# Layer 0 scan: half of the inputs from the eighth state on made by TensorE, an eighth by GpSimd

## The reference

```
def step(h, inp):
    u_t, dt_t, B_t, C_t = inp
    dA = jnp.exp(-dt_t[..., None] * A)
    h = dA * h + (dt_t * u_t)[..., None] * B_t[:, None, :]
    y = jnp.einsum('bdn,bn->bd', h, C_t)
    return (h, y)
```

## Time and profile before

| | |
|---|---|
| median of 3 runs | 1251.55 us (1249.97 to 1255.73) |
| the profiled execution | 1258.5 us |
| its span | 1257.2 us |
| mean granted PE clock | 0.861 of full speed |
| first scan instruction starts at | 84.5 us of the span |
| last scan instruction starts at | 311.5 us |
| busy over the span | PE 915.5, DVE 899.7, ACT 578.6, POOL 547.4 us |

### The profile page before, as it was taken

How to read it: one execution, slowest core, us unless ns; L and a number is a source line. 1 busy time by engine, 2 the same in 40 slices (tenths; PEclk the granted TensorE clock), 3 DMA queues, 4 the chain that set the end, 5 groups by cost and what they waited for, 6 DMA issues and landing times.

```text
span 1257.2 us, 18690 instructions
## 1 busy us (share of the span) xinstructions
PE 915.5 (73%) x5207; PEld 533.2 (42%) x5207; DVE 899.7 (72%) x1700; ACT 578.6 (46%) x1232; POOL 547.4 (44%) x553
## 2 busy tenths in 40 slices
PE   6977787888666866678889888679893850558782
PEld 3522234333344552222223322469893530547682
DVE  6679999999999377877887871754455589972223
ACT  3478663665132443146776668334342740223232
POOL 2068995999401323201112211245534585235643
PEclk9879898999877988679998999679996775669896
DMA  8000000000000301311110100511102000011113
GB/s 294 1 1 1 1 0 1 1 1 1 1 0 1 134 1 53 98 27 27 27 28 27 27 2 2 201 62 35 39 27 78 1 0 1 9 42 36 41 33 113
DMA packets 28018, 46.32 MB, mean 37 GB/s; under 512 B 8721, under 2 KB 16409, under 8 KB 26897
## 3 DMA queue, kind: packets, MB, share of 16 engines
q1 hardware_dynamic: 22672, 34.67, 8.6%
q0 software_dynamic: 4096, 8.35, 2.2%
q10 hardware_dynamic: 1152, 2.10, 0.4%
HBM read 34.46 MB, written 12.58 MB: 37 GB/s over the span
## 4 chain that ended last, share of the span: by engine, by line
PE 39%; DVE 30%; issue 11%; ACT 8%; POOL 5%; DMA 3%; another core or an unknown queue 2%; SPq 1%; DVEq 0%; ACTq 0%; POOLq 0%
PE ps L2798 9%; PE ps L2807 5%; PE ps L1821 5%; PE ps L1803 4%; DVE sb_hs L756 3%; POOL sb_gs L926 3%; DVE sb_l_mxp L1935 2%; PE ps L1748 2%; DVE sb_xn L168 2%; DVE sb_stats L145 2%; ACT sb_l_rc L2228 1%; PE ps L1756 1%; ACT sb_l_pT L1878 1%; DVE ps L718 1%
## 5 line engine op out<-in xcount | busy, mean ns | idle before, releaser
L1935 DVE TENSOR_REDUCE sb_l_mxp<-ps 128x2 f32<-128x1024 f32 (+3 forms) x152 | 171.5, 1163 | 41.5 <-PE ps L1748 40.2
L926 POOL TENSOR_TENSOR sb_gs<-sb_hs,sb_xp 128x512 f32<-128x512 f32 x128 | 163.2, 1294 | 23.2 <-DVE sb_hs L756 21.1
L1878 ACT ACTIVATE sb_l_pT<-ps 128x512 f32<-128x512 f32 (+3 forms) x256 | 111.4, 521 | 76.8 <-PE ps L1803 75.7
L2798 PE MATMUL ps<-sb_hT,sb_f_shared 128*128 x936 | 127.5, 288 | 13.6 <-ACT sb_f_shared L2815 6.8
L605 PE MATMUL ps<-sb_gs,sb_ident 128*128 128x512 f32 x256 | 133.8, 605 | 1.0 <-POOL sb_gs L926 0.7
L2798 PEld LDWEIGHTS ps<-sb_hT,sb_f_shared 128*128 128x128 f32 x936 | 116.6, 200 | 22.2 <-issue 22.2
L2868 DVE SCALAR_TENSOR_TENSOR sb_f_rows<-ps,sb_f_mask,sb_f_rows 128x128 f32 x78 | 27.4, 351 | 116.6 <-PE ps L2807 57.0
L1803 PE MATMUL ps<-sb_l_qk 51*128 51x512 bf16 (+3 forms) x384 | 89.3, 335 | 19.0 <-ACT sb_l_pT L1878 7.8
L2896 POOL DMA_INDIRECT moe_y<-sb_f_rows,sb_f_rowi x64 | 63.8, 997 | 82.4 <-DVE sb_f_rows L2868 69.7
L2807 PE MATMUL ps<-sb_sw_f_out,sb_f_hid 128*128 x624 | 86.3, 283 | 14.0 <-ACT sb_f_hid L2837 9.3
L2837 ACT ACTIVATE sb_f_hid<-ps 128x512 f32<-128x512 f32 x78 | 46.5, 596 | 103.3 <-PE ps L2798 75.9
(11 more groups left out here) (394 smaller groups left out, 2046.8 us busy)
## 6 DMA issues: line engine op xcount, KB each, us to landing
sb_sw_f_in<-w_f_in SPq DMA_DIRECT2D x2, 2048.0 KB, 10.1
sb_sw_f_out<-w_f_out SPq DMA_DIRECT2D x2, 2048.0 KB, 13.1
sb_l_qk<-spill SPq DMA_DIRECT2D x112, 32.0 KB
spill<-sb_l_parts SPq DMA_DIRECT2D x12, 256.0 KB, 2.9
moe_y<-c_f_zero SPq DMA_DIRECT2D x1, 2048.0 KB, 9.8
sb_sw_f_up<-w_f_up SPq DMA_DIRECT2D x1, 2048.0 KB, 12.1
moe_h<-sb_f_rows SPq DMA_DIRECT2D x8, 256.0 KB, 5.2
sb_f_rows<-moe_y SPq DMA_DIRECT2D x8, 256.0 KB, 6.1
```

The costliest lines, as they stand in the source:

```text
L926: gp.tensor_tensor(gs[:, q % SL, :], hs[:, q % SL, :], cs[:, k % 2, hf * CH:(hf + 1) * CH], ALU.mult).then_inc(times_c, 1)
L1878: ac.activation(pT[e % 3][:, h, 0:width], ps[:, bank[n_bank], 0:width], ACT.Exp, scale=L2_SCALE).then_inc(exped, 1)
L1935: dv.tensor_reduce(dst, src, AX_X, ALU.max).then_inc(max_out, 1)
L2798: m = pe.matmul(ps[:, 2 * (i % 2) + n, fs], own[:, i % 2, n, fs], xr[:, bass.ds(r, 1), :], start=True, stop=True)
```

## The change

It concerns only who makes the input of a step.

- Rounds 0 to 6 stay as they are.
- From round 7 (the eighth state) on, the steps of the second half of the tokens (hf = 1, two of four in each round) get their input from PE. Once for each sequence, PE turns dtu of the second half, and the B rows, so that tokens lie on partitions: 3 more uses of bank 3 for each sequence (`turned_b`, `turned_dtu`), at iterations 16 to 18 and 40 to 42, each copied out by ACT into `bT` and `dtuT`. Two rounds ahead, ACT multiplies each of the four tiles of `dtuT` (128 tokens x 256 channels) by the column of B of that state, a scale for each partition (`scale_tile`), into one of three buffers `scaled`. PE then transposes four 128x128 tiles of it into the step's PSUM bank (`product`), in the place where `b_row` stood.
- POOL makes the input of one step in eight: step 2 of each odd round (e = 1, hf = 0), issued after its product of step 2 of the round before. `gin` and `brows` have one buffer instead of two.
- DVE makes the rest: two inputs in an even round, one in an odd one.

Nothing else is changed; the scan, the products with C and the accumulation stay.

```
+        T_FROM = 7
+        HF_T = CPB - 1
+        def gp_step(k):
+            if k < T_FROM:
+                return per_n - 1
+            return per_n - 2 if k % 2 else None
...
+        def by_tensor(q):
+            return q // per_n >= T_FROM and steps[q][3] == HF_T
...
+        TURN_AT = {16: ("b", 0), 17: (0, 0), 18: (0, 1), 40: ("b", 1), 41: (1, 0), 42: (1, 1)}
+        def rows_at(q):
+            k, r = divmod(q, per_n)
+            keys = []
+            if k + 1 < B * DS:
+                if r < CPB:
+                    keys.append(("c", k + 1, r))
+                elif r == CPB and k + 1 in gp_at:
+                    keys.append(("gp", k + 1))
+            if q in TURN_AT:
+                keys.append(("turn",) + TURN_AT[q])
+            return keys
...
+            def turned_dtu(b, e):
+                pe.wait_ge(dt_out, DT[b] + 2)
+                for t in range(TPC):
+                    t0 = b * S + HF_T * CH + t * P
+                    i = pe.transpose(ps[:, 3, t * P:(t + 1) * P], dtu[:, e, t0:t0 + P], ident[:])
+                return i
...
+            def product(q):
+                b, n, e, hf = steps[q]
+                k = q // per_n
+                pe.wait_ge(scanned, q - NB_ + 1)
+                pe.wait_ge(tiles_scaled, TPC * (k - T_FROM + 1))
+                for t in range(TPC):
+                    i = pe.transpose(ps[:, q % NB_, t * P:(t + 1) * P], scaled[k % 3][:, t, e * P:(e + 1) * P], ident[:])
+                i.then_inc(turned_in, 1)
...
             for q in range(NQ + LAG):
-                if NB_ <= q + 2 < NQ and not by_gpsimd(q + 2):
+                if NB_ <= q + 2 < NQ and by_vector(q + 2):
                     b_row(q + 2)
-                k, r = divmod(q, per_n)
-                if r < ROW3 and k + 1 < B * DS:
-                    bank3 = c_row(k + 1, r)
+                if q + 2 < NQ and by_tensor(q + 2):
+                    product(q + 2)
+                for key in rows_at(q):
+                    bank3 = bank3_row(key)
...
+            def scale_tile(k, t):
+                b, n = divmod(k, DS)
+                ac.wait_ge(crow, row_count[("turn", b, ET - 1)])
+                if k >= T_FROM + 3:
+                    ac.wait_ge(turned_in, so_far(by_tensor, (k - 2) * per_n - 1))
+                ac.activation(scaled[k % 3][:, t, :], dtuT[:, b, t].rearrange("p e d -> p (e d)"), ACT.Copy,
+                              scale=bT[:, b, t, n:n + 1]).then_inc(tiles_scaled, 1)
...
             for q in range(NQ):
                 if q + 2 < NQ and q != LN_AT + 1:
                     decay(q + 2)
-                k, r = divmod(q, per_n)
-                if r < ROW3 and k + 1 < B * DS:
-                    c_row(k + 1, r)
+                k, t = divmod(q, per_n)
+                if T_FROM <= k + 2 < B * DS:
+                    scale_tile(k + 2, t)
+                for key in rows_at(q):
+                    bank3_row(key)
...
             for q, (b, n, e, hf) in enumerate(steps):
...
-                if by_gpsimd(q) and k + 1 < B * DS:
+                if k + 1 in gp_at and q % per_n == gp_step(k + 1):
                     multiply(k + 1)
```

More of the change, by code:

```diff
@@ L392, in layer0_mixer @@
         cs = free[:, 0:2 * S].rearrange("p (z n) -> p z n", z=2)
-        brows = free[:, 2 * S:2 * S + 2 * CH].rearrange("p (z n) -> p z n", z=2)
-        gin = free[:, 2 * S + 2 * CH:2 * S + 4 * CH].rearrange("p (z n) -> p z n", z=2)
+        brows, gin = free[:, 2 * S:2 * S + CH], free[:, 2 * S + CH:2 * S + 2 * CH]
+        dtuT = hT[:].rearrange("p (b t e d) -> p b t e d", b=B, t=TPC, e=ET)
+        bT = xn[:].rearrange("p t d -> p (t d)")[:, 0:B * TPC * DS].rearrange("p (b t n) -> p b t n", b=B, n=DS)
+        scaled2 = sb("scaled", [P, 2, TPC, ET * P], ctx=ctx)
+        tiles = lambda a: a.rearrange("p (t n) -> p t n", t=TPC)
+        scaled = [scaled2[:, 0], scaled2[:, 1], tiles(free[:, 2 * S + 2 * CH:2 * S + 4 * CH])]
         xz_mm, xz_x, xz_z = sem("xz_mm"), sem("xz_x"), sem("xz_z")
@@ L440, in by_gpsimd, with by_vector, so_far @@
         def by_gpsimd(q):
-            return q % per_n == per_n - 1
-        def nth(q):
-            return (per_n - 1) * (q // per_n) + q % per_n
+            return q % per_n == gp_step(q // per_n)
+        def by_tensor(q):
+            return q // per_n >= T_FROM and steps[q][3] == HF_T
+        def by_vector(q):
+            return not by_gpsimd(q) and not by_tensor(q)
+        def so_far(made, q):
+            return sum(1 for i in range(q + 1) if made(i))
+        gp_rounds = [k for k in range(B * DS) if gp_step(k) is not None]
+        gp_at = {k: j for j, k in enumerate(gp_rounds)}
+        TURN_AT = {16: ("b", 0), 17: (0, 0), 18: (0, 1), 40: ("b", 1), 41: (1, 0), 42: (1, 1)}
+        first_rows = [("c", 0, 0), ("c", 0, 1), ("gp", 0)]
+        def rows_at(q):
[9 more added lines that the diff above has]
+            return keys
+        row_order = first_rows + [key for q in range(NQ) for key in rows_at(q)]
+        row_count = {key: j + 1 for j, key in enumerate(row_order)}
         EXP_AT, LN_AT = {1: CPB, 3: CPB + 1}, 9
@@ new lines, in bank3_row @@
+            def bank3_row(key):
+                pe.wait_ge(*bank3)
+                if key[0] == "c":
+                    b, n = divmod(key[1], DS)
+                    i = spread(DS + n, b, key[2])
+                elif key[0] == "gp":
+                    b, n, e, hf = steps[key[1] * per_n + gp_step(key[1])]
+                    i = spread(n, b, hf)
+                elif key[1] == "b":
+                    i = turned_b(key[2])
+                else:
+                    i = turned_dtu(key[1], key[2])
+                i.then_inc(crow_mm, 1)
+                return crow, row_count[key]
@@ L739, in vector_scan @@
                     rows_dt(1)
-                if q + 1 < NQ and not by_gpsimd(q + 1):
+                if q + 1 < NQ and by_vector(q + 1):
                     multiply(q + 1)
@@ L909, in multiply @@
             def multiply(k):
-                b, n, e, hf = steps[k * per_n + per_n - 1]
+                b, n, e, hf = steps[k * per_n + gp_step(k)]
                 t0 = b * S + hf * CH
-                gp.wait_ge(crow, ROW3 * (k + 1))
+                j = gp_at[k]
+                gp.wait_ge(crow, row_count[("gp", k)])
                 gp.wait_ge(dt_out, DT[b] + 2)
-                if k >= 2:
-                    gp.wait_ge(scanned, (k - 1) * per_n)
-                gp.tensor_tensor(gin[:, k % 2, :], dtu[:, e, t0:t0 + CH], brows[:, k % 2, :],
+                if j >= 1:
+                    before = gp_rounds[j - 1]
+                    gp.wait_ge(scanned, before * per_n + gp_step(before) + 1)
+                gp.tensor_tensor(gin, dtu[:, e, t0:t0 + CH], brows,
                                  ALU.mult).then_inc(gp_inputs, 1)
```

63 lines of the change are left out of this document (39 added, 24 removed).

## The result

| | before | after |
|---|---|---|
| median of 16 runs each | 1255.62 us | 1250.24 us (1245.32 to 1256.0) |
| ratio after / before | | 0.9965, 95% interval 0.9948 to 0.9982 |
| the profiled execution | 1258.5 us | 1247.78 us |
| its span, mean granted PE clock | 1257.2 us, 0.861 | 1246.5 us, 0.867 |
| first to last scan instruction | 226.94 us | 224.21 us |

The changed kernel is faster by 0.35% of 1255.6, or 4.4 us (2.2 to 6.5). The forecast was 4.0 us, with "within 0.5%" as the likeliest case. The forecast median of 1247.5 us went out from 1251.55 us before; with 16 runs that yardstick itself came to 1255.62, so the difference is what compares, not the median. The two profiled executions lie 10.7 us apart, but only 2.73 of that lies in the scan; the rest is in code that the change doesn't touch.

What follows compares the result with a forecast made beforehand. DVE was taken to set the pace at 6.36 us a round, POOL close behind. Terms: -9.2 + 0.1 + 3.9 + 0.7 + 0.2 + 0.3 = -4.0 us, median 1251.55 to 1247.5; range 1239 to 1253, 8 times in 10.

Steps and rivals of the forecast that it cites:

- within 0.5%: Whole kernel: the median differs from before by no more than 0.5%, 6.3 us; chance 0.56.
- a chain that the change leaves in place: Scan: loop from POOL's last product through C row copy, PE, DVE multiply and scan back to POOL; 5.55 us.
- the first rival: Scan rounds: work alone decides, 5.56 us a round, kernel 1237.5 to 1240; 0.38 together with something between.
- I add 0.1: Even rounds from round 11: POOL's input waits for the B row copy, lengthening 6.18 to 6.28 us.
- Rounds 21 and 23: POOL's deviations in rounds 20 and 22 cost 2.4 us now and 2.6 afterwards: +0.2 us.
- The signs: Profile after: rounds near 6.2 and 5.6, DVE not full, POOL full in even rounds, round 10 some 10 us.
- three signs of being wrong: POOL waits for DVE in odd rounds outside the chain, round 10 under 8 us, or clock falls somewhere new.
- Round 10: Clip and three turned tiles contend for bank 3: 10.3 us against 6.36, +3.9 us.
- Rounds 7 to 9: ACT's gz clips, hidden before, show beside the scaling: sum 19.2 against 19.1, +0.1 us.
- The rival of 1.00 us a product: PE's four transposes cost 1.00 us: PE 6.32 a round, +4.4, 1256 us; chance 0.04 of the 0.56.
- The rival of a dearer copy: ACT's scaled copy costs 0.5 instead of 0.40: a round 6.0, kernel 1251 us; chance included in 0.56.
- the rival was the right thing to fear: PE's granted clock falls: one fall +2 us, slower by 0.5% from five, 1258; chance above 1257.8 is 0.06.

Runs made afterwards that it cites:

- three C buffers in the kernel before: Kernel before the change, given a third buffer for the C rows from round 8 on: 1.0002 of before.
- three C buffers: Changed kernel with three buffers for the C rows from round 8 on instead of two, the copy's wait one round further back: 0.9904 of before.
- the start at round 11: Changed kernel with a third C row buffer, PE's inputs from round 11 instead of 7, turned tiles at iterations 23, 27, 31, 43, 47, 51: 0.9873 of before.
- tiles apart: Changed kernel with turned tiles at iterations 11, 15, 19, 43, 47, 51, which have no other bank 3 row, instead of 16-18 and 40-42: 0.9934 of before.
- without the eighth: Changed kernel with POOL making no input from round 7 on; DVE makes both first-half inputs in every round: 0.9876 of before.
- accumulation first: Changed kernel with PE's accumulation of step q - 3 issued ahead of the bank 3 row of iteration q instead of behind it: 0.9917 of before.
- the first four experiments: Changed kernel with, singly: no POOL input from round 7, 0.9876; third C row buffer, 0.9904; turned tiles spread, 0.9934; no scaled copies, 0.9945 of before.
- the next four: Changed kernel again, 0.9972; accumulation ahead of bank 3 row, 0.9917; before with third C row buffer, 1.0002; changed with that buffer and spread tiles, 0.9870.
- the last three: Changed kernel, tiles spread, with: no POOL input from round 7, 0.9861; third C row buffer and accumulation ahead, 0.9884; that buffer and PE inputs from round 11, 0.9873.

## Why the prediction was right, and where it was off

The total was 4.0 us by forecast and 4.4 (2.2 to 6.5) by the runs. The mechanism, a chain that the change leaves in place, holds. That the two totals lie so close is in part luck: by the profile the scan gained 2.7 us and not 4.0, since the even rounds were sized too low, and round 6, round 10 and round 23 paid for a part of that.

- **What bounded the kernel before** was DVE's work. Shown: DVE is busy for the whole of rounds 8 to 15, and three C buffers in the kernel before leave its rounds at 6.36.
- **The chain sets odd rounds.** Forecast 2.84 + 1.35 + 1.36 = 5.55 us from copy to copy; measured 2.76 + 1.35 + 1.37 = 5.48 (283.37 to 288.85). Shown from two sides: a third C buffer or a shorter chain brings the pair to the work that DVE and POOL have (11.18 and 11.26). This also rules out the first rival, work alone at 5.56 a round, for the kernel as changed: it is the time of the kernel *with* the third buffer (5.59 a round).
- **Even rounds were mis-sized.** The step was "in an even round POOL's five products set 6.18; I add 0.1, as POOL's input waits for the B row copy", 6.28. Measured from copy to copy 6.57 (276.80 to 283.37). POOL's input at 280.77 did not wait for the copy; what POOL waited for was DVE, 0.37 us before 278.30. The odd round's chain has let POOL run out of work, so that it meets each scan as it comes, and two scans with a multiply between them are 276.95 - 275.26 = 1.69 apart where a product takes 1.235. I had treated the two kinds of round as independent, with five products back to back. 6.18 + 0.37 = 6.55. Followed through both rounds the pair is one loop, and the first fence has every link: 2.76 from copy to scan (283.37 to 286.13), then the next two scans with a multiply between them, 1.19 (to 287.32) and 1.69 (as 275.26 to 276.95), 1.35 to POOL's product (278.30), 3.70 to its last product of the round (282.00), 1.37 to the copy (283.37). That makes 12.06, and POOL's input, the eighth, is a link of it. The pair came to 12.06 instead of 11.83; over ten pairs that is 2.3 of the 2.4 us by which rounds 11 to 31 fell short (-6.3 against -8.7). So close a match is in part chance: round 11 took 6.73 where 5.92 was counted and rounds 16 to 19 gained 0.5 us where 1.5 was counted, while rounds 20 to 23 gained 1.9 where 1.6 was.
- **Rounds 21 and 23** were taken to cost 2.4 us more than their neighbours before and 2.6 after. After the change they cost 1.8 (7.21 and 7.23 against 6.30). Round 23 took 8.45 us before at a granted clock of 0.80, and after the change it ran at 1.00; with three C buffers in the kernel before it took 6.36, at 1.00 too. So a part of the 2.09 us that the forecast put down to POOL was PE's clock, which it carried over as if it were a fixed cost. How large a part is not shown.
- **The signs** named ahead: POOL was to be full in even rounds and DVE no longer full, but DVE is full in them and POOL waits. None of the three signs of being wrong came: POOL's wait in odd rounds is the chain's (0.52 us before 287.48), round 10 took over 8 us, and from round 7 on the granted clock is 0.97 or more in every round but round 16 (0.92, and 0.83 before).
- **Round 10** was foreseen at 10.3 and took 9.25, but round 11 took 6.73: 15.98 together, against 10.3 + 5.9 = 16.2. The order of the waits was as followed. The fence below shows them: PE waits 1.82 for ACT's copy, then 1.15, ACT 0.75 for PE, POOL 2.06, DVE 3.38. The tiles apart take rounds 10 to 12 from 21.74 to 18.91. The clock is a cost of its own here: with three C buffers it fell in round 10 (0.84) and the round took 10.37.
- **Rounds 7 to 9** took 19.94 against 19.2 forecast and 19.1 before: +0.9 instead of +0.1. Without the scaled copies they take 18.85, so ACT's work there, clip and scaling together, shows more than I held, in rounds 8 and 9 (round 7 stays at 6.80). It shows only together with the chain: with ACT's work unchanged they take 18.26 with three C buffers and 17.88 without the eighth.
- **Not foreseen:** round 6 became 1.1 us shorter (6.91 to 5.79), since the input of the second step of round 7, whose multiply (0.58 of DVE) stood ahead of the scan that ends round 6, is no longer DVE's. That multiply had also waited 0.44 us for its B row (at 138.08), with PE at a granted clock of 0.56 from 136 to 139 us; this pays for the +0.86 of round 4 (forecast +0.7). With the start at round 11 the round is back at 6.90.
- **PE.** Four transposes took 0.60 us, as forecast, at a clock of 1.00 in the steady rounds. The Trainium skill, "TensorE: Matmul & The Clock Gate", Part 4, gives some 275 ns for a transpose: by that, the trace agrees in the length of one record (mean 275) and not in the pace, since four end within 0.60 us. The rival of 1.00 us a product did not come, and neither did the 8 us of loss that I had estimated from the page's figure.
- **ACT.** The scaled copy's record is 500 ns long (forecast 490), and without any of them the pair does not change. What follows it on ACT starts 0.40 us after it (134.96 to 135.36), as taken. The rival of a dearer copy is out.
- **PE's clock** did not fall in the steady rounds, but the rival was the right thing to fear: it fell in round 10 without the eighth (0.62) and with three C buffers (0.84), in round 21 without the scaled copies (0.79) and in rounds 3, 7 and 23 with the tiles apart (0.79).

The changed kernel in round 10, in order of time (604 and 612 turn the B rows and dtu):

```profile
161.41 0.29 PE L604 MATMUL ps<-sb_sel,sb_bc 96*128 96x16 bf16 x4 [1.82 <-ACT sb_xp L957]
164.45 0.66 PE L612 MATMUL ps<-sb_ident,sb_mod_space 128*128 128x128 f32 x4 [1.15 <-ACT sb_xp L957]
165.14 0.60 ACT L957 ACTIVATE sb_hT<-ps 128x512 f32<-128x512 f32 x1 [0.75 <-PE ps L612]
166.14 1.27 POOL L1023 TENSOR_TENSOR sb_gs<-sb_hs,sb_xp 128x512 f32<-128x512 f32 x1 [2.06 <-PE ps L680]
166.22 0.70 DVE L793 TENSOR_TENSOR ps<-sb_mod_space,ps 128x512 f32<-128x512 f32 x1 [3.38 <-PE ps L645]
```

Where the rest of the gain went, then: a pair at 12.06 instead of 11.18 costs 8.8 us over the ten pairs of rounds 12 to 31, which is the wait for the C buffer, and the turned tiles in a row cost 2.8 in rounds 10 to 12. Together 11.6; the kernel without either has a scan 10.7 us shorter. The two kernels with the tiles apart and one of the two cures of the chain (the third buffer, or no eighth) are at 0.9861 and 0.9870, some four times the gain of the change. Their intervals don't tell them apart, and both beat the kernel before and the changed one.

One thing stays open: the timed gain of most kernels is larger than that of their scan (no eighth 1.24% or 15 us against 9.6; accumulation first 0.83% or 10 against 6.0; the changed kernel 4.4 against 2.7). One profiled execution each doesn't show where the remaining 1 to 6 us lie, and no run was made for it. The profiles show how far such a difference can be chance: from the last scan instruction on, where the code of all these kernels is the same, the first four experiments took 913 to 918 us, the next four 939 to 942 and the last three 937 to 944.

## What to carry to other kernels

When work is taken off the engine that sets the pace, the work of each engine gives only a floor: write down the longest loop that runs through a single buffer as well (here copy, row, accumulation, row, multiply, scan, product: 5.5 us under a round of 6.36) and compare the new round with it. An engine that is second in line (POOL at 56.0 of 57.9 us) is a poor place for an eighth of the work, as long as its work is a link of that loop: with two C buffers the pair of rounds was 0.54 us shorter with that eighth on the busiest engine, with three it was 0.34 us longer so (11.52 against 11.18). Cut the loop or take the work out of it; either gave about the same time here (0.9870 and 0.9861). And extra uses of a buffer with one slot (bank 3) belong in the iterations that have none, one at a time; here round 10 fell from 9.25 us to 5.9 to 6.0 so, though in the first trial of it rounds 3, 7 and 23, at a lower granted clock, took 3.1 us more in the profiled execution.

## What the runs showed of the hardware

- The granted clock does not follow from one wait. PE waited 1.82 us in round 10 of the changed kernel and the clock stayed at 1.00. It waited 1.83 in the same place with three C buffers, and the round had 0.84 and took 1.1 us more; it waited 1.73 without the eighth, and the stretch had 0.62 and the round took 2.1 us more. The transposes and accumulations that followed took about twice as long (1.06 against 0.60 for four transposes, 1.91 and more against 1.02 to 1.10 for an accumulation). What makes the difference is left open. The lines are from round 10 with three C buffers; the changed kernel's stand above.

```profile
160.39 0.29 PE L605 MATMUL ps<-sb_sel,sb_bc 96*128 96x16 bf16 x4 [1.83 <-ACT sb_xn L958]
160.52 2.05 PE L681 MATMUL ps<-sb_gs,sb_ident 128*128 128x512 f32 x2
162.36 1.06 PE L638 MATMUL ps<-sb_ident,sb_scaled 128*128 128x128 f32 x4
```

- A transpose of 128x128 f32 leaves one record, an accumulation of 128x512 f32 two; four of the first take 0.60 us, one of the second 1.02. So an input made by transposes is cheaper on PE than the step's accumulation.
- The same kernel differs by about 2% from one group of runs to another (1231 us and 1253 to 1256 for the kernel before), some five times the effect of the change. Whether that is the chip or something else is not shown.
